# Two reorderings at the head of a dense aggregation: three small products on TensorE, one DMA issue on ScalarE

## The reference, cut to what matters

```python
def ref(x, edge_index, W, envW, envb):          # L=2 layers, K=4 experts
    row, col = edge_index[0], edge_index[1]
    z = x
    for l in range(2):
        weights = softmax(z @ envW[l] + envb[l])
        agg = scatter_mean(z[col], row, N)       # mean over the incoming edges
        combined = concatenate([agg, z], axis=-1)
        outputs = einsum('nd,kdo->nko', combined, W[l]) + z[:, None, :]
        z = relu(einsum('nk,nko->no', weights, outputs))
    return z
h = maximum(layernorm(x), 0)
out = x + ref(h, stack([src, dst]), W, envW, envb)
```

## Time and profile before

| | |
|---|---|
| median of three runs | 1801.98 us (1800.79 to 1802.11) |
| the profiled execution, own time | 1797.94 us |
| its span, first to last instruction | 1795.80 us |
| TensorE busy | 1577.5 us, 88% |
| GpSimd busy | 1202.2 us, 67% |
| VectorE busy | 888.8 us, 49% |
| ScalarE busy | 572.7 us, 32% |
| mean granted TensorE clock | 0.981 of full speed |

### The profile page before, as it was taken

The page is one execution under the profiler, slowest core; times in us unless marked ns, Lnnn a source line. Parts: engine busy times, 40 slices in busy tenths (PEclk is TensorE's granted clock), DMA queues, the critical chain, the costliest instruction groups (busy, mean ns, idle before and its releaser), DMA issues. The chain is left out here.

```text
span 1795.8 us, 36215 instructions
## 1 busy us (share of the span) xinstructions
PE 1577.5 (88%) x8502; PEld 1112.0 (62%) x8503; DVE 888.8 (49%) x2026; ACT 572.7 (32%) x1254; POOL 1202.2 (67%) x1187
## 2 busy tenths in 40 slices
PE   1059999999999999999993699999999999999998
PEld 1036666666766666676661476666666666666665
DVE  6665555566555656656553233333333343334433
ACT  4414434433443443334431022222222222222222
POOL 1377777677677767667762776667766666666764
PEclk9989999999999999999996799999999999999999
DMA  7877777666676666667767976777777777777775
GB/s 218 281 225 225 218 221 213 202 193 199 205 217 205 206 202 199 189 200 212 216 206 281 372 227 199 217 230 230 211 218 220 221 220 220 220 224 213 221 221 147
DMA packets 160203, 393.35 MB, mean 219 GB/s; under 512 B 36989, under 2 KB 61080, under 8 KB 160180
## 3 DMA queue, kind: packets, MB, share of 16 engines
q0 software_dynamic: 92544, 302.70, 56.5%
q10 hardware_dynamic: 35112, 61.46, 9.7%
q1 hardware_dynamic: 32524, 28.91, 5.2%
HBM read 347.61 MB, written 45.37 MB: 219 GB/s over the span
## 5 line engine op out<-in xcount | busy, mean ns | idle before, releaser
L713 POOL DMA_INDIRECT ring<-zp_dram,gather_idx x1152 | 1184.0, 1028 | 504.8 <-issue 275.0
L1340 PE MATMUL agg_ps<-zp,stage 128*128 128x258 f32 x1568 | 448.1, 323 | 26.5 <-PEq L101 26.5
L1373 PE MATMUL mix_ps<-w_sb,turned_z 128*128 128x512 f32 x784 | 402.1, 612 | 17.1 <-PEq L101 17.1
L1302 PE MATMUL agg_ps<-ring,onehot 128*128 x1248 | 390.6, 341 | 27.0 <-PEq L101 21.8
L1373 PE MATMUL mix_ps<-w_sb,turned_m 128*128 128x512 f32 x784 | 393.1, 601 | 16.0 <-PEq L101 14.8
L1342 PE MATMUL agg_ps<-zp,stage 128*128 128x256 f32 x1568 | 385.3, 282 | 0.0
L1080 ACT ACTIVATE stage<-counts_sb 128x512 fp32r<-128x512 uint8 (+1 forms) x416 | 247.2, 605 | 392.9 <-ACTq L101 391.9
L1340 PEld LDWEIGHTS agg_ps<-zp,stage 128*128 128x128 f32 x1568 | 296.6, 189 | 91.2 <-issue 87.4
L1307 PE MATMUL agg_ps<-ring,onehot 128*128 x1248 | 322.8, 285 | 0.0
L1342 PEld LDWEIGHTS agg_ps<-zp,stage 128*128 128x128 f32 x1568 | 296.9, 189 | 34.6 <-issue 34.6
L866 DVE TENSOR_TENSOR onehot<-nodes,dst_t 128x512 fp32r<-128x512 f32 (+1 forms) x396 | 224.1, 600 | 165.5 <-issue 141.8
(11 more groups left out here) (157 smaller groups left out, 898.5 us busy)
## 6 DMA issues: line engine op xcount, KB each, us to landing
ring<-zp_dram,gather_idx POOLq DMA_INDIRECT x1152, 3.8
zp_dram<-zp SPq DMA_DIRECT2D x7, 1792.0 KB, 7.2
a_dram<-counts_sb ACTq DMA_DIRECT2D x16, 784.0 KB
zp_dram<-parts ACTq DMA_DIRECT2D x49, 256.0 KB, 3.8
zp<-zp_dram SPq DMA_DIRECT2D x4, 1792.0 KB, 15.5
counts_sb<-a_dram ACTq DMA_DIRECT2D x17, 400.0 KB
parts<-in_x ACTq DMA_DIRECT2D x48, 128.0 KB
counts_sb<-a_dram ACTq DMA_DIRECT2D x16, 384.0 KB
```

The costliest lines, as they stand in the source:

```text
L713: pool.indirect_dma_start(out=ring[:, k, t, 0:2 * D].bitcast(F32), out_offset=None, in_=zp_dram[l], in_offset=bass.IndirectOffsetOnAxis(ap ...
L1302: mm = pe.matmul(agg_ps[:, bank, 0:D + 2], onehot[:, place, t, :], rows[:, :, D:2 * D + 2], start=place == 0 and t == 0, stop=True, skip_g ...
L1340: pe.matmul(agg_ps[:, bank, 0:D + 2], stage[:, g % 2, i, :], zp[:, c, D:2 * D + 2], start=c == 0, stop=True, skip_group_check=True)
L1373: mm = pe.matmul(mix_ps[i][:, :], (turned_z, turned_m)[what][:, c, :], w[:, i * HALF:(i + 1) * HALF], start=what == 0 and c == 0, stop=wha ...
```

## The change

On TensorE `pair(3)`, `pair(4)` and `pair(5)` of the first slot each go one place further forward relative to the products: before `product(6)`, before `product(7)`, and behind it. The same instructions are issued. On ScalarE `store_counts` goes behind `fill_stage(0)` and `fill_stage(1)`. Layer 1 keeps its order.

```diff
@@ scalar, slot k == 0
                                     if first:
                                         for j in range(3, PAIRS_IN[1]):
                                             move_pair(1, j)
-                                        store_counts(dn)
                                     else:
                                         take(act, s_ald, PER_ROUND * 16)
                                     for g in range(2):
                                         fill_stage(g)
+                                    if first:
+                                        store_counts(dn)
@@ tensor, first_slot
                         pair(2)
                         turn_z()
+                        pair(3)
                         product(6).then_inc(s_agg, 1)
-                        pair(3)
+                        pair(4)
                         product(7)
-                        pair(4)
                         pair(5)
```

## The result

| | before | after |
|---|---|---|
| median | 1801.38 us (4 runs, 1798.79 to 1802.11) | 1786.93 us (4 runs, 1785.59 to 1789.71) |
| ratio of the runs, 95% interval | | 0.9933 [0.9921, 0.9945] |
| span of the profiled execution | 1795.8 us | 1787.6 us |

The ratio is 12.1 us less, 9.9 to 14.2 by its interval. The two profiled executions differ by only 8.2 us: the one of before took 1797.94 us, less than any of its four runs, and the one of after is the slowest of its four.

What follows compares the result with a forecast made beforehand. TensorE was taken to set the pace, waiting for ScalarE before the dense sum; 0.44 (store) plus 0.31 (pairs) made 0.75 us in 15 rounds, plus 0.60 in the first: 11.9 us, 1790 us, range 1785.5 to 1796.

Steps and rivals of the forecast that it cites:

- The sum: Dense sum's start in layer 0: 0.75 us gained in each of 15 rounds, 0.60 in the first, together 11.9 us.
- What bounds: TensorE, busy 88%, sets the pace; time comes only from its waits, here 0.65 us before the dense sum, awaiting ScalarE.
- The store: ScalarE's chain before the dense sum: issuing the store behind two widenings removes 0.44 us a round, bounds 0.34 to 0.49.
- The pairs: ScalarE's moves 3 to 5 no longer wait for their pairs, so move 5 comes 0.31 us earlier a round.
- The ceiling of 0.90 us: TensorE before the dense sum: 0.90 us lost a round, counted by the pitch of starts, limits any gain.
- The covers: Slack against new waits: product(2) wanted 1.2 us after begin's start or the second mixing, pair(5) covered by 0.11 us.
- Everything else moves along: Behind the dense sum's start, TensorE's other waits hang on its own earlier work through DVE and ScalarE, and shift with it.
- The likeliest case: Store and pairs together gain 0.60 to 0.85 us a round, 9.6 to 13.6 us, 1788.4 to 1792.4; 68%.
- the whole wait goes: Shorter ScalarE gaps make TensorE's own work the bound at the dense sum: 14.4 us or a little less, 1787.6; 10%.
- Only the store counts: Moves keep their times because copy_z holds move 3, not its pair: 7.0 us gained, 1795.0; 12%.
- Slower, since the store lands too late: Late landing makes ScalarE hold move 0 of the rest slot: 15.4 us lost, 1817; 3%.
- Given back: GpSimd sets the round, or the wait returns at the next product needing a one-hot: 1802; 7%.

Runs made afterwards that it cites:

- product6_first: The changed kernel with product(6) moved ahead of pair(2) and pair(4) behind product(7): 1789.98 us, ratio 0.9945 to the kernel before.
- reload_early: The changed kernel, SyncE reloading layer 1's features on one signal from ScalarE instead of counting off 16 rounds: 1783.12 us, ratio 0.9907 to the kernel before.
- store_late: The changed kernel with the store's issue moved to the end of the dense slot, behind the last copy_z: 1787.78 us, ratio 0.9928 to the kernel before.
- pairs_only: The kernel before with only the three pairs moved forward, the store staying ahead of the widenings: 1794.93 us, ratio 0.9971.
- early_regs: The changed kernel, DVE keeping the next block's unit numbers in registers, last one-hots ahead of the loads: 1767.58 us, ratio 0.9819 to the kernel before.
- early_regs_and_reload: The changed kernel with DVE's unit numbers in registers and SyncE's earlier reload without the counting: 1766.68 us, ratio 0.9805 to the kernel before.

## Why the prediction was right, and where it was not

Forecast were 1790.0 us in a range of 1785.5 to 1796, and faster with 0.90; measured were 1786.93 us and a ratio that stands for 12.1 us less, where 11.9 were forecast. That agreement is partly luck. The sum has a term that was too small by a quarter (0.75 for 0.98 us a round) and lacks another of the opposite sign.

- *What bounds.* Right in the main: TensorE's waits, and ScalarE's chain in front of the first dense product. That time "can come only out of its waits" was too narrow: of the 14.7 us between the dense starts 10.2 are idle time, and 4.5 are products that stand closer. The wait in front of the dense sum went in all 16 rounds, and no other of its size came up inside them. `product6_first` shows that the chain is the bound still.
- *The store, forecast 0.44 us a round.* The mechanism is right, the size 0.50: the step from the last move to the first widening is 0.64 us, where I had 0.70. The error is the gap behind an instruction of ScalarE, 0.27 us and not 0.32. I had 0.27 as the shortest gap in the rows and set it as the bound. Where the issue went is not as forecast either: it starts at 501.50, beside the first widening and ahead of the second (501.78), and not behind both. That is 4.30 us behind `turn_z`, where it was 504.44 - 499.89 = 4.55. So against `turn_z` the store goes out 0.25 us earlier than before, not 0.96 later. In the old place the issue stands behind move 5, and `move_pair` waits for its own end, so ScalarE is idle during it (0.76 us in front of the widening). Behind a widening nothing waits for that end, and the issue ran while ScalarE worked.
- *The pairs, forecast 0.31 us a round.* The mechanism is right, the size 0.48. Move 3 follows `copy_z` after 0.28 us, where the first round had shown 0.37, and move 4 follows move 3 after 0.84, where I took 0.92 from a pair of moves that differ. Move 5 keeps its 0.92. The right pitch stood in the trace of before, in the prologue, whose last four moves find their pairs ready. Move 3 starts 119.09 - 118.25 = 0.84 us behind move 2, and the last, move 6, 121.71 - 120.79 = 0.92 behind move 5:

```profile
119.09 0.58 ACT L1094 ACTIVATE counts_sb<-win_ps 128x490 uint8<-128x490 f32 x1 [0.27 <-ACTq L101]
...
120.79 0.58 ACT L1094 ACTIVATE counts_sb<-win_ps 128x490 uint8<-128x490 f32 x1 [0.27 <-ACTq L101]
121.71 0.66 ACT L1094 ACTIVATE counts_sb<-win_ps 128x490 uint8<-128x490 f32 x1 [0.33 <-ACTq L101]
```

- *The ceiling of 0.90 us.* Wrong as a ceiling: the gain is 0.98. I had kept TensorE's own work fixed ("the logits start where they do now"). But from `turn_z` to `product(0)` it is 500.18 - 497.20 = 2.98 us, where it was 503.07 - 499.89 = 3.18. Two pairs in a row and the logits behind them take 503.07 - 502.07 = 1.00 us; one pair there takes 500.18 - 499.60 = 0.58, and the other, between two products, 0.21. By this work the dense sum could start at 500.18 + 1.72 = 501.90, and it starts at 502.02, so ScalarE is last by 0.12, where I had 0.15.
- *The covers.* They held. `begin` starts 0.87 us ahead of `product(2)` (503.36 and 504.23), where I had 1.2. `pair(5)`, with 0.11 us of forecast cover, did not wait. The second mixing of DVE is 0.22 us later against `turn_z`, as forecast.
- *"Everything else moves along".* This step failed. It held for the rounds and not for the boundary between the layers, where the last gather comes one place later, and the reload, the weights and layer 1 behind it. From the last dense start to the end it is 876.7 and 875.5 us in the two profiles of before and 879.9 and 879.6 in those of after, so 3.6 us are given back. I saw that GpSimd has slack in a round, and did not look at what else hangs on its last gather. `reload_early` shows that an earlier reload shortens this stretch. That the gathers fall one place behind because the rounds are shorter is argued only, and it is not the whole rule: `store_late` has rounds of the changed kernel's length and is two places behind. The reload, 1.3 us later, accounts for about half of the 3.6 us. The cause of the rest, inside layer 1, stays open.
- *The sum as it was.* The first dense start to the last is 775.0 and 775.2 us before, 760.4 and 760.6 after: 14.65. The first round adds some 0.5, not the 0.60 forecast: from `turn_z` it was 5.82 and 6.36 us before and is 5.44 and 5.70. 15.1 - 3.6 = 11.5 us by the profiles, beside 12.1 and 13.5 by the two ratios.
- *The rivals.* The likeliest case had 0.60 to 0.85 us in a round, and 0.98 is above it. What happened in the rounds is nearer to "the whole wait goes": the gaps were the short ones and the work packed closer, worth 15.1 us where that case had 14.4 "or a little less". It differs in that ScalarE is still the last, by 0.12 us. Only the loss at the boundary brought the time back to the likeliest case. "Only the store counts" is refuted by `pairs_only`. "Slower, since the store lands too late" is refuted by far: issued 18.5 us later still it costs nothing that can be measured, and has landed within 5.7 us. The Trainium skill (DMA: Bandwidth & Descriptors, Rules for kernel authors) would have a DMA issued early. The runs agree with it where somebody waits for the landing: the reload of `reload_early`, issued 6.8 us earlier, shortened the stretch behind it by 8.5. For the store, which has landed long before ScalarE asks for it, they say that the place of the issue matters and the hour of the landing does not. "Given back" happened in part, at a place that I had not named.

## What to carry to other kernels

When one engine waits for a chain on another, write down the pitch of every step of that chain, with its wait already satisfied, and take the shortest seen for the same pair of instructions, with the semaphore instructions between them; a step that ends a wait says nothing of its own pitch. An issue of a DMA on the engine that feeds the bound belongs behind the work that the bound waits for, as long as the landing has room. Here 0.34 us of issue were 0.50 in the chain, where the queue had waited for the instruction before it, and nothing behind a widening. And a gain in a loop has to be followed out of the loop: the queue that runs at its own pace (here the last gathers) does not get faster, and whatever counts on its last item can pay at the end.

## What the runs showed of the hardware that was not expected

- ScalarE's pitch depends on more than the instruction: with its pair ready, a move follows the one before after 0.84 us in one place and after 0.92 in another (move 4 behind move 3, and move 5 behind move 4), to 0.01 us in nearly all rounds. In the code the slow ones are those with one more instruction in front: move 1 and the last of a group first give `s_keyfree`. In the prologue it is the same, 0.92 for moves 1 and 6 and 0.84 to 0.85 for moves 3, 4 and 5. So one semaphore instruction is worth some 0.08 us in this chain, an estimate from these rows; no run leaves it out.
- The issue of the store takes 0.34 us in every place. Behind a move that waits for its own end it cost the chain 0.50 us; behind a widening it ran at 501.50 while ScalarE worked until 501.87 (501.24 + 0.63), and cost it nothing.
- Three loads of registers from SBUF and their arithmetic held DVE for 2.31 us ahead of one-hots that need 1.04 us. With one load gone and two moved behind the one-hots 0.05 us are left there and 0.89 us stand behind. This edit brought more than the change under study: 19 us by the medians.
- GpSimd's gathers stand 1.25 us apart when nothing holds them, and rounds shorter by 0.5 or by 1.0 us show at the end as one gather, 1.2 us, in both cases. What decides between one and two (24.5 us in `store_late`, `early_regs` and `early_regs_and_reload`) was not found.
